# A two-layer cross-attention and feed-forward kernel: its first stage in another order, and GpSimd's first query splits moved

## The chip, the cores and the metric

The kernel runs on one core of one Trainium2 chip. The metric is the device time of one execution in microseconds (us); lower is better. The core has TensorE (PE; its weight loads are shown apart as PEld), VectorE (DVE), ScalarE (ACT), GpSimd (POOL) and SyncE (SP, which here only issues DMAs). Each takes its own instructions in the order in which they are written and waits on semaphores that the program names.

## The reference, cut to what matters

```python
x = x + fake_quant(layernorm(x)) @ fake_quant(ctx)                      # first attention, 0..255 levels
x = x + mx_linear(silu(mx_linear(ln(x), w_gate)) * mx_linear(ln(x), w_up), w_down)   # fp6 rows, fp4 weights, blocks of 32
x = x + attention(ln(x) @ wq, rope(ctx @ wk), ctx @ wv, mask) @ wo       # 32 query heads, 8 key heads of 128
x = x + (silu(ln(x) @ gate * s) * (ln(x) @ up * s)) @ down * s
```

x is 2 x 256 x 512, ctx is 2 x 512 x 512, the inner width of both feed-forward layers is 1376 (padded to 1408), everything float32.

## The kernel before, in words

The keys and values of the second attention depend on ctx alone, so they fill TensorE in the first stage, while the other engines quantise.

**Stage one** (to about 130 us). TensorE computes 27 units of keys and values: `("k", i, b)` is key head i for batch b, `("v", i, h)` is 128 context rows i by 512 columns h; a unit is four float32 matmuls of 128x512. The table STEPS (L39) names them in order, as a first and a second part of each of 8 steps. Their results go round three PSUM banks (5, 6, 7; `rotation`, `take`, L269 and L462): a unit can begin when the unit three places before it has been copied out by ScalarE (`copy_keys`, `copy_values`) and from there SP stores it to DRAM. Beside that the 33 weight tiles of the first feed-forward layer (gate, up, down) are quantised to fp4 in 9 chunks, 8 of four tiles and a last one of one tile. For chunk i: SP `mx_load(i)`; DVE `mx_peaks`, `mx_exponents`; POOL `scale_in(i)`; ACT `mx_lift(i, 0)` and `(i, 1)`; DVE `mx_round(i, 0)`, `(i, 1)`, `mx_clip(i)`; POOL `scale_out(i)`, which lets TensorE transpose the chunk in two halves (`mx_turn(i, 0)`, `(i, 1)`, L491) that ACT keeps in WT (`mx_keep`). The rows of x go through `quantise_rows` (a layernorm on DVE), `rows_scale`, `clip_rows`, `rows_keep`; the context through `context_scale`, `clip_context`, `context_keep`; `attention0(b)` is the first attention for batch b. Then DVE normalises the result (`layernorm`), `fp6` quantises it, POOL's `fp6_out` writes it, TensorE turns it (`turn_quantised(1)`) and ACT keeps it. The key head 0 needs its rotary embedding at once: ACT copies the swapped halves out (`swap`), DVE multiplies by the cosine in PSUM (`key_cosine`), POOL by the sine (`key_sine`), DVE adds (`key_rotate`). The other heads are rotated later.

**Stage two** (about 132 to 184 us) is the first feed-forward layer for four row tiles t: TensorE `gate_up(t)` in three slices c (PSUM banks 4 to 7 in pairs, so that slice n waits until DVE has read slice n-2), ACT `silu(t)`, DVE `inter_products(t)` and `inter_quantise(t)` (fp6 again), POOL `fp6_out`, TensorE `turn_inter(t)`, ACT `keep_inter(t)`, TensorE `down(t)`, DVE `add_down(t)`. Five key units that stage one has no room for (LATE_KEYS) are put in its gaps as `late_keys(n, parts)`; late_keys(3) computes head 7, batch 0, and stands between the transposes of row tiles 2 and 3 (`turn_rows`, L622). It waits for `wk_in`, the load of that head's weights, `k_load(7)` (L421). DVE's last layernorm normalises tiles 0 to 2 and then tile 3.

**Stage three** (from 185 us) is the second attention, one software pipeline over units U; POOL splits each query weight in a high and a low part (`split`, L1070; `wqh_ready`, `wq_split`), and SP loads head h of wq only after `wq_split` has reached h-1 (two raw buffers). SP's queue at the end of stage two reads, in this order:

```python
            wq_load(2, 0)
            wq_load(3, 1)
            k_load(7)
            for i, b in LATE_KEYS[:4]:
                key_store(i, b)
            sp.wait_ge(ffn0_done, NT)
```

with `after(sp, wq_split, h - 1)` inside wq_load. The fourth layer (660 us on) is the last feed-forward.

## Time and profile before

| | us |
|---|---|
| median of 3 runs | 709.29 (708.45 to 712.96) |
| the profiled execution, its own time | 712.11 |
| its span from the first to the last recorded instruction | 710.0 |
| busy in the span: PE, DVE, POOL, ACT | 672.4, 525.8, 457.6, 362.8 |

2.1 us of the execution's own time lie around the span. Row times below are in us from the span's start, the duration follows the start, and brackets at a row's end give the idle time before it and what ended it. A group "x8" is several instructions of one kind in a row.

### The profile page before, as it was taken

What the parts mean: (1) busy time and instruction counts of PE and PEld (TensorE: products, weight loads), DVE (VectorE), ACT (ScalarE), POOL (GpSimd) and SP (SyncE); (2) the same over time, 40 slices, a digit from 0 to 9 for tenths busy, and PEclk for the clock granted to TensorE, in tenths of its full rate; (3) what the DMA queues carried; (4) which work ended last, traced back from release to release, by engine and by line L of the source; (5) the groups of instructions that cost most, each with busy time, mean ns of one, the idle gap of its engine ahead of it and who ended that gap; (6) DMA issues with size and microseconds to landing.
All of it is one profiled execution on the core that took longest, in us unless ns stands there. A gap on an engine that the chain in (4) does not pass through costs nothing.

```text
span 710.0 us, 10983 instructions
## 1 busy us (share of the span) xinstructions
PE 672.4 (95%) x3099; PEld 494.8 (70%) x3104; DVE 525.8 (74%) x1039; ACT 362.8 (51%) x684; POOL 457.6 (64%) x401
## 2 busy tenths in 40 slices
PE   4989899899989999999999999999999999699998
PEld 2434344444566788888888888888888887588886
DVE  4977799778678888888889888888888885631113
ACT  2659444542466666665665665565665663211111
POOL 2365716424269879778878779689688554556661
PEclk9989999999999999999999999999999999999999
DMA  9885322140232113023132141221221021122221
GB/s 338 274 309 184 127 90 75 45 163 18 98 109 80 68 61 118 31 66 112 30 101 77 37 126 44 83 80 44 88 74 40 21 65 55 54 81 89 89 89 60
DMA packets 39402, 67.25 MB, mean 95 GB/s; under 512 B 3664, under 2 KB 11984, under 8 KB 38352
## 3 DMA queue, kind: packets, MB, share of 16 engines
q1 hardware_dynamic: 39376, 66.93, 28.8%
q8 instruction: 13, 0.21, 0.1%
q14 instruction: 13, 0.11, 0.0%
HBM read 57.48 MB, written 9.44 MB: 94 GB/s over the span
## 4 chain that ended last, share of the span: by engine, by line
PE 77%; DVE 10%; issue 4%; POOL 4%; ACT 3%; DMA 1%; SPq 0%; POOLq 0%; ACTq 0%; DVEq 0%
PE ps L635 16%; PE ps L637 16%; PE ps L636 16%; PE ps L703 11%; PE ps L668 7%; PE ps L503 4%; PE ps L519 4%; PE ps L566 2%; DMA X<-in_x 1%; DVE mx_amax L1244 1%; DVE mx_raw L1262 1%; DVE f L1292 1%; DVE f_amax L1287 1%; POOL wq_sb L1074 1%; PE ps L497 1%
## 5 line engine op out<-in xcount | busy, mean ns | idle before, releaser
L1083 POOL TENSOR_SCALAR prob<-prob,rinv 128x512 f32<-128x512 f32 x128 | 89.4, 699 | 79.3 <-DVE rinv L1420 79.3
L944 ACT ACTIVATE prob<-ps,nmax 128x512 f32<-128x512 f32 x128 | 88.3, 690 | 97.4 <-DVE nmax L1413 94.9
L703 PE MATMUL ps<-xt,wq_sb 128*128 128x512 f32 x384 | 103.2, 393 | 3.8 <-DVE q_cos L1428 2.1
L955 ACT CAST pT<-ps 128x512 fp32r<-128x512 f32 x128 | 75.1, 587 | 52.0 <-PE ps L668 51.0
L1413 DVE CUSTOM_DVE_ANT_0 ps<-ps,mask_sb 128x512 f32<-128x512 f32 x128 | 87.9, 686 | 6.7 <-PE ps L637 6.3
L1434 DVE TENSOR_TENSOR pT<-ps,pT 128x512 fp32r<-128x512 f32 x128 | 86.3, 674 | 2.6 <-ACT pT L955 1.7
L703 PEld LDWEIGHTS ps<-xt,wq_sb 128*128 128x128 f32 x384 | 71.6, 188 | 21.9 <-issue 4.6
L668 PE MATMUL ps<-idf,prob 128*128 128x128 f32 x512 | 76.7, 272 | 0.3 <-POOL prob L1083 0.3
L668 PEld LDWEIGHTS ps<-idf,prob 128*128 128x128 f32 x512 | 63.8, 141 | 17.0 <-POOL prob L1083 1.0
L503 PE MATMUL ps<-ctxT,wk_sb 128*128 128x512 f32 x128 | 63.4, 636 | 7.7 <-DMA ctxT<-in_ctx_cols 6.7
L1035 POOL TENSOR_TENSOR mx_raw<-mx_raw,mx_r 128x2048 f32<-128x2048 f32 (+1 forms) x9 | 30.2, 3354 | 61.4 <-DVE mx_r L1252 61.4
L519 PE MATMUL ps<-wv_sb,ctxT 128*128 128x512 f32 x128 | 58.8, 610 | 5.3 <-DVE col L1228 2.8
L635 PE MATMUL ps<-pT,vt 128*128 128x512 f32 x128 | 61.1, 477 | 0.5 <-DVE pT L1434 0.5
L1086 POOL TENSOR_TENSOR q_swp<-q_swp,ropeQ 128x512 f32<-128x512 f32 x32 | 47.1, 1472 | 17.6 <-ACT q_swp L965 17.6
L1470 DVE SCALAR_TENSOR_TENSOR int<-ps,sc,silu 128x512 f32<-128x512 f32 x11 | 8.2, 750 | 59.6 <-PE ps L637 59.6
L635 PE MATMUL ps<-wo_sb,oT 128*128 128x512 f32 x128 | 50.2, 393 | 1.7 <-DVE oT L1401 1.4
L635 PE MATMUL ps<-kt,qt 128*128 128x512 f32 x128 | 50.6, 395 | 0.9 <-DVE kt L1447 0.5
L637 PE MATMUL ps<-pT,vt 128*128 128x512 f32 x128 | 50.8, 397 | 0.0
L636 PE MATMUL ps<-pT,vt 128*128 128x512 f32 x128 | 50.3, 393 | 0.0
L637 PE MATMUL ps<-kt,qt 128*128 128x512 f32 x128 | 50.2, 392 | 0.0
L1074 POOL TENSOR_TENSOR wo_sb<-wo_raw,wo_sb 128x512 fp32r<-128x512 f32 x32 | 48.4, 1511 | 2.7
L636 PE MATMUL ps<-wo_sb,oT 128*128 128x512 f32 x128 | 50.0, 391 | 0.0
(152 smaller groups left out, 1572.2 us busy)
## 6 DMA issues: line engine op xcount, KB each, us to landing
mx_raw<-in_mxw SPq DMA_DIRECT2D x8, 1024.0 KB, 6.7
wq_raw<-in_wq SPq DMA_DIRECT2D x32, 256.0 KB, 3.1
wo_raw<-in_wo SPq DMA_DIRECT2D x32, 256.0 KB, 2.7
k_scr<-k_st SPq DMA_DIRECT2D x16, 256.0 KB, 2.0
v_scr<-v_st SPq DMA_DIRECT2D x16, 256.0 KB, 2.3
kr<-k_scr SPq DMA_DIRECT2D x16, 256.0 KB, 2.9
vr<-v_scr SPq DMA_DIRECT2D x16, 256.0 KB, 3.7
kr_swp<-k_scr SPq DMA_DIRECT2D x28, 128.0 KB, 3.3
```

The source lines that it names most:

```text
L503: last = mm(bank(n), wk_sb[:, i % 2, k], ctxT[:, k, b * CTX:(b + 1) * CTX], start=(k == 0), stop=(k == KD - 1))
L519: last = mm(bank(n), ctxT[:, k, i * P:(i + 1) * P], wv_sb[:, k, h * 512:(h + 1) * 512], start=(k == 0), stop=(k == KD - 1))
L635: mm(out_ap, left[0], right[0], start=first, stop=False)
L636: mm(out_ap, left[0], right[1], start=False, stop=False)
L637: return mm(out_ap, left[1], right[0], start=False, stop=final)
L668: last = nc.tensor.transpose(bank(2 + i % 2)[:, k * P:(k + 1) * P], prob[:, i, k * P:(k + 1) * P], idf[:])
L703: last = mm(query_bank(H), wq_sb[:, par, l, k], xt[:, r, k], start=(n == 0), stop=(n == 11))
L944: nc.scalar.activation(prob[:, j], bank(j % 2), ACT.Exp, bias=nmax[:, j:j + 1], scale=-1.0, accum_out=rsum[:, j:j + 1]).then_inc(exps, 1)
L955: copy(pT[:, v % 2, 0, :, i * P:(i + 1) * P], bank(2 + i % 2).rearrange("p (k c) -> p k c", k=4)).then_inc(ph_ready, 1)
L1083: nc.gpsimd.tensor_scalar(prob[:, i], prob[:, i], rinv[:, i:i + 1], 1.0, ALU.mult, ALU.mult).then_inc(probs, 1)
L1413: nc.vector.tensor_tensor_reduce(out=bank(j % 2), in0=bank(j % 2), in1=mask_sb[:, 2 * (u % 2) + j % 2], scale=-1.0, scalar=BIG, op0=ALU.ad ...
L1434: tt(pT[:, v % 2, 1, :, i * P:(i + 1) * P], bank(2 + i % 2).rearrange("p (k c) -> p k c", k=4), pT[:, v % 2, 0, :, i * P:(i + 1) * P].bitc ...
```

## The change

It has four parts.

1. **Loads.** SP issues x and the first half of wv ahead of the first weight chunk, then chunks 0 and 1, and the context rows as two loads of 1 MB (`ctx_load`) in place of one of 2 MB. DVE does quantise_rows before mx_peaks(0).
2. **Banks, units and the first key head.** STEPS is written anew: step 1 has four units, the last step has two, and its second part is empty. The rotation of key head 0 goes from DVE and PSUM to POOL and SBUF: ACT makes one more copy (`k_own`), which frees the PSUM bank, and POOL does all three operations (`key_rotate`, one for each batch); the result has its own buffer and its own store.
3. **Gate and up ahead of chunk 6.** In step 7 no chunk is transposed; mx_turn(6, 0), (6, 1) come behind gate_up(0), and mx_turn(7, 0), (7, 1), (8, 0) behind gate_up(1). POOL does the fp6_out of the rows before scale_out(6), DVE does mx_round(8, 0) before mx_clip(7), and attention0 before the peaks of a chunk.
4. **GpSimd's query splits.** The split of query head 0 goes ahead of the last fp6_out of stage two. Behind it POOL waits for `ln_ready` 12, which is the last row tile's normalisation, before it splits head 1. late_keys(2) gives one of its four parts to the place ahead of down(3), and three behind it, where it was two and two.

```diff
-    ([("v", 0, 1), ("v", 1, 1)], [("k", 1, 0)]),
-    ([("k", 1, 1), ("v", 2, 1)], [("k", 2, 0)]),
...
-    ([("v", 7, 0), ("v", 7, 1)], [("k", 5, 0)]),
+    ([("v", 0, 1), ("v", 1, 1), ("k", 1, 0)], [("k", 1, 1)]),
+    ([("v", 2, 1), ("k", 2, 0)], [("v", 3, 1)]),
...
+    ([("v", 7, 1), ("k", 5, 0)], []),
...
             k_load(0)
             ctxT_load(0)
-            mx_load(0)
             sp.dma_start(X[:], x.rearrange("(t p) d -> p t d", p=P)).then_inc(x_in, 16)
             sp.dma_start(sc[:], scalars).then_inc(sc_in, 16)
             wv_load(0)
+            mx_load(0)
+            mx_load(1)
             sp.dma_start(idf[:], ident).then_inc(id_in, 16)
-            mx_load(1)
+            ctxT_load(1)
             sp.dma_start(ropeK[:], rope_k).then_inc(rk_in, 16)
-            ctxT_load(1)
+            wv_load(1)
             mx_load(2)
-            wv_load(1)
             k_load(1)
-            key_store(0, 0)
+            ctx_load(0)
...
-                if i > 0:
+                if 0 < i < NFULL - 1:
                     mx_turn(i - 1, 0)
...
             gate_up(0)
+            mx_turn(NFULL - 2, 0)
+            mx_turn(NFULL - 2, 1)
+            gate_up(1)
+            mx_turn(NFULL - 1, 0)
             late_keys(0, range(0, 2))
-            mx_turn(NFULL - 1, 0)
             mx_turn(NFULL - 1, 1)
-            gate_up(1)
             mx_turn(NFULL, 0)
             late_keys(0, range(2, 4))
...
             turn_inter(NT - 1)
-            late_keys(2, range(0, 2))
+            late_keys(2, range(0, 1))
             down(NT - 1)
-            late_keys(2, range(2, 4))
+            late_keys(2, range(1, 4))
...
             swap(0)
+            copy_values(0, 0)
+            copy_values(1, 0)
             mx_lift(0, 0)
             mx_lift(0, 1)
+            rows_scale()
+            copy_values(2, 0)
...
             mx_lift(1, 1)
+            swap(1)
             rows_keep()
-            swap(1)
...
+            def key_rotate(b):
+                if b == 0:
+                    pool.wait_ge(rk_in, 16)
                 pool.wait_ge(k_swapped, b + 1)
+                pool.wait_ge(*keys_out(0, b))
                 tt(k_swp[:, b], k_swp[:, b], ropeK[:, 1], ALU.mult).then_inc(k_sined, 1)
+                tt(k_own[:, b], k_own[:, b], ropeK[:, 0], ALU.mult).then_inc(k_cosed, 1)
+                pool.wait_ge(k_sined, b + 1)
+                pool.wait_ge(k_cosed, b + 1)
+                tt(k_own[:, b], k_own[:, b], k_swp[:, b], ALU.add).then_inc(k_roped, 1)
...
-                scale_out(i)
                 if i == L0_AT + 2:
                     fp6_out(q1[:].rearrange("p t d -> p (t d)"), NT * D, 0, q1_ready)
+                scale_out(i)
+                if i == 0:
+                    key_rotate(1)
             scale_out(NFULL)
...
+            for t in range(NT):
+                if t == NT - 1:
+                    pool.wait_ge(wq_in[0], 16)
+                    split(wq_sb[:, 0, 0], wq_sb[:, 0, 1], wq_raw[:, 0], wqh_ready, wq_split, 1)
+                after(pool, intq_turned, t - 1)
+                fp6_out(int_q[:, t % 2], IPAD, t + 1, intq_ready)
...
-            pool.wait_ge(wq_in[0], 16)
-            split(wq_sb[:, 0, 0], wq_sb[:, 0, 1], wq_raw[:, 0], wqh_ready, wq_split, 1)
+            pool.wait_ge(ln_ready, 3 * NT)
             pool.wait_ge(rq_in, 16)
```

POOL at the end of stage two, before (int_q is written by fp6_out, wq_sb by a split):

```order
L1046 TENSOR_TENSOR int_q<-f6c,f_e 128x1408 [waits f6_clipped,intq_turned] x2
L1072 TENSOR_SCALAR wq_sb<-wq_raw 128x512 [waits wq_in0]
L1074 TENSOR_TENSOR wq_sb<-wq_raw,wq_sb 128x512 [waits wqh_ready]
L1072 TENSOR_SCALAR wq_sb<-wq_raw 128x512 [waits rq_in,wq_in1]
L1074 TENSOR_TENSOR wq_sb<-wq_raw,wq_sb 128x512 [waits wqh_ready]
```

and now:

```order
L1069 TENSOR_TENSOR int_q<-f6c,f_e 128x1408 [waits f6_clipped,intq_turned]
L1097 TENSOR_SCALAR wq_sb<-wq_raw 128x512 [waits wq_in0]
L1099 TENSOR_TENSOR wq_sb<-wq_raw,wq_sb 128x512 [waits wqh_ready]
L1069 TENSOR_TENSOR int_q<-f6c,f_e 128x1408 [waits f6_clipped,intq_turned]
L1097 TENSOR_SCALAR wq_sb<-wq_raw 128x512 [waits wq_in1,ln_ready,rq_in]
L1099 TENSOR_TENSOR wq_sb<-wq_raw,wq_sb 128x512 [waits wqh_ready]
```

The first split has moved ahead of the last int_q, and the second now waits for ln_ready as well. SP at the same place stands as it did (this is the new kernel; wk_sb is k_load(7), the two wq_raw are heads 2 and 3):

```order
L389 DMA wq_raw<-in_wq 128x512 [waits wq_split] x2
L319 DMA wk_sb<-in_wk 128x512 [waits k_sums]
L324 DMA k_scr<-k_st 128x512 [waits k_copied] x4
L389 DMA wq_raw<-in_wq 128x512 [waits wq_split,ffn0_done]
L394 DMA wo_raw<-in_wo 128x512
```

Nothing moved on it. TensorE from the first gate_up on, before (L566 is gate_up, L503 a key part, L497 mx_turn):

```order
L566 MATMUL ps<-WT,q1T 128x384 [waits inter_ready]
L566 MATMUL ps<-WT,q1T 128x384 x7
L503 MATMUL ps<-ctxT,wk_sb 128x512 [waits wk_in1]
L503 MATMUL ps<-ctxT,wk_sb 128x512
L497 MATMUL ps<-idb,mx_w 128x128 [waits mx_kept,mx_ready]
L497 MATMUL ps<-idb,mx_w 128x128 x7
L497 MATMUL ps<-idb,mx_w 128x128 [waits mx_kept,mx_ready]
L497 MATMUL ps<-idb,mx_w 128x128 x7
L566 MATMUL ps<-WT,q1T 128x512 [waits inter_ready]
```

and now, from the last slice of gate_up(1) (L577 is gate_up, L513 a key part, L507 mx_turn, L585 turn_inter):

```order
L577 MATMUL ps<-WT,q1T 128x384 [waits inter_ready]
L577 MATMUL ps<-WT,q1T 128x384 x7
L507 MATMUL ps<-idb,mx_w 128x128 [waits mx_kept,mx_ready]
L507 MATMUL ps<-idb,mx_w 128x128 x7
L513 MATMUL ps<-ctxT,wk_sb 128x512 [waits wk_in1]
L513 MATMUL ps<-ctxT,wk_sb 128x512
L507 MATMUL ps<-idb,mx_w 128x128 [waits mx_kept,mx_ready]
L507 MATMUL ps<-idb,mx_w 128x128 x7
L507 MATMUL ps<-idb,mx_w 128x128 [waits mx_kept,mx_ready]
L507 MATMUL ps<-idb,mx_w 128x128 x3
L513 MATMUL ps<-ctxT,wk_sb 128x512 x2
L585 MATMUL ps<-idb,int_q 128x128 [waits intq_ready,mx_kept]
```

What stood between gate_up(0) and gate_up(1), a half of late_keys(0) and chunk 7, now stands between gate_up(1) and turn_inter(0).

## Rows read from the trace of the kernel before

**Rows 1.** Stretches: length, busy of PE, PEld, DVE, ACT, POOL, PEclk, DMA, GB/s.

```profile
0.00:130.00 130.00, 114.54 (x382) 53.25 (x384) 104.81 (x150) 67.24 (x80) 64.09 (x25) 0.96 0.56 193
...
44.00:46.00 2.00, 2.00 (x3) 0.67 (x2) 1.19 (x1) 0.00 (x0) 0.00 (x0) 0.50 0.86 246
```

**Rows 2.** TensorE's timeline in stage one, each row behind a wait; the last is gate_up(0).

```profile
6.65 5.75 PE L503 MATMUL ps<-ctxT,wk_sb 128*128 128x512 f32 x8 [6.65 <-DMA ctxT<-in_ctx_cols]
14.84 14.00 PE L519 MATMUL ps<-wv_sb,ctxT 128*128 128x512 f32 x32 [2.44 <-DMA wv_sb<-in_wv]
...
41.42 0.91 PE L497 MATMUL ps<-idb,mx_w 128*128 128x128 bf16 x8 [2.29 <-POOL mx_w L1041]
43.34 6.19 PE L503 MATMUL ps<-ctxT,wk_sb 128*128 128x512 f32 x8 [1.01 <-DVE k_st L1282]
...
79.12 5.37 PE L519 MATMUL ps<-wv_sb,ctxT 128*128 128x512 f32 x8 [2.81 <-DVE col L1228]
...
132.07 4.93 PE L566 MATMUL ps<-WT,q1T 128*128 128x512 bf16 x24 [2.09 <-ACT q1T L790]
```

**Rows 3.** GpSimd's timeline: scale_in(2), scale_out(0); scale_out(6), the rows' fp6_out.

```profile
34.03 3.64 POOL L1035 TENSOR_TENSOR mx_raw<-mx_raw,mx_r 128x2048 f32<-128x2048 f32 x1 [6.59 <-DVE mx_r L1252]
37.64 3.64 POOL L1041 TENSOR_TENSOR mx_w<-mx_q,mx_e 128x2048 bf16<-128x2048 bf16 x1
...
119.92 3.64 POOL L1041 TENSOR_TENSOR mx_w<-mx_q,mx_e 128x2048 bf16<-128x2048 bf16 x1
123.52 3.64 POOL L1046 TENSOR_TENSOR q<-f6c,f_e 128x2048 bf16<-128x2048 bf16 x1
```

**Rows 4.** VectorE in stage two: the first products of row tiles 1 and 2.

```profile
143.35 0.69 DVE L1345 TENSOR_TENSOR int<-silu,ps 128x512 f32<-128x512 f32 x1
...
151.96 1.27 DVE L1345 TENSOR_TENSOR int<-silu,ps 128x512 f32<-128x512 f32 x2
```

**Rows 5.** VectorE's last layernorm: a step beside a split; tile 3, first and last.

```profile
175.02 1.12 DVE L1184 TENSOR_TENSOR newton<-newton,var_eps 128x3 f32<-128x3 f32 x1
...
178.92 0.68 DVE L1354 TENSOR_TENSOR X<-ps,X 128x512 f32<-128x512 f32 x1
...
182.70 0.55 DVE L1187 TENSOR_SCALAR xhat<-X,meanvar,rstd 128x512 f32<-128x512 f32 x1
```

**Rows 6.** TensorE's timeline: late_keys(3), then the transposes of tile 3.

```profile
180.11 3.60 PE L503 MATMUL ps<-ctxT,wk_sb 128*128 128x512 f32 x8
183.54 0.60 PE L629 MATMUL ps<-idf,xhat 128*128 128x128 f32 x4
```

**Rows 7.** VectorE's timeline: the starts of two layernorms, then mx_clip(7) and mx_clip(8).

```profile
11.99 2.47 DVE L1165 BATCH_NORM_STATS2 stats<-X 128x6 f32<-128x512 f32 x4 [0.21 <-DMA X<-in_x]
...
97.83 2.47 DVE L1165 BATCH_NORM_STATS2 stats<-X 128x6 f32<-128x512 f32 x4
...
123.65 4.06 DVE L1270 TENSOR_SCALAR mx_q<-mx_q 128x2048 bf16<-128x2048 bf16 x1
...
129.07 2.51 DVE L1270 TENSOR_SCALAR mx_q<-mx_q 128x512 bf16<-128x512 bf16 x1
```

**Rows 8.** Timelines in stage two: mx_turn(7, 1), its copy on ScalarE, turn_inter(0).

```profile
140.35 0.61 PE L497 MATMUL ps<-idb,mx_w 128*128 128x128 bf16 x8 [1.19 <-ACT WT L820]
...
140.99 1.01 ACT L820 COPY WT<-ps 128x1024 bf16<-128x1024 bf16 x1 [0.79 <-PE ps L497]
...
147.54 0.78 PE L574 MATMUL ps<-idb,int_q 128*128 128x128 bf16 x11
```

**Rows 9.** Timelines of GpSimd's second split and of SP; DMAs from 176.4 us: KB, us to landing.

```profile
174.16 0.62 POOL L1072 TENSOR_SCALAR wq_sb<-wq_raw 128x512 fp32r<-128x512 f32 x1
174.85 1.27 POOL L1074 TENSOR_TENSOR wq_sb<-wq_raw,wq_sb 128x512 fp32r<-128x512 f32 x1
...
176.52 0.43 SPq L317 DMA_DIRECT2D wk_sb<-in_wk  x1
...
wk_sb<-in_wk SPq DMA_DIRECT2D x1, 256.0 KB, 3.1
```

More of the change, by code:

```diff
@@ L208, in build @@
             res = sb("res", [P, NT, D], F32, a)
-        x_in, id_in, sc_in, ctx_in = sem("x_in"), sem("id_in"), sem("sc_in"), sem("ctx_in")
+        x_in, id_in, sc_in = sem("x_in"), sem("id_in"), sem("sc_in")
+        ctx_in = [sem(f"ctx_in{i}") for i in range(2)]
         ctxT_in = [sem(f"ctxT_in{i}") for i in range(2)]
@@ L285, in keys_out @@
         def keys_out(i, b):
-            n = 2 * i + b
-            return (k_roped, n + 1) if i == 0 else (k_copied, n - 1)
+            return k_copied, 2 * i + b + 1
         def drained(unit):
@@ L342, in wv_load, with ctx_load @@
                              wv[:, n * 512:(n + 1) * 512].rearrange("(k p) c -> p k c", p=P)).then_inc(wv_in[n], 16)
+            def ctx_load(b):
+                rows = slice(b * CTX, (b + 1) * CTX)
+                sp.dma_start(ctx_f[:, 4 * b:4 * b + 4], ctx_rows[rows, :].rearrange("(t p) d -> p t d", p=P)).then_inc(ctx_in[b], 16)
             k_load(0)
             ctxT_load(0)
-            mx_load(0)
             sp.dma_start(X[:], x.rearrange("(t p) d -> p t d", p=P)).then_inc(x_in, 16)
@@ L366, in _ @@
                     mx_load(i + NRAW)
+                if i == 1:
+                    for b in range(2):
+                        sp.wait_ge(k_roped, b + 1)
+                        sp.dma_start(k_scr[0, b], k_own[:, b]).then_inc(k0_stored, 16)
                 stores(STEPS[i][0] + STEPS[i][1])
@@ L805, in swap @@
                 act.wait_ge(k_sums, b + 1)
-                n = 0 if b == 0 else rotating(("k", 0, b))
+                n = key_bank(0, b)
                 copy(k_swp[0:64, b], ps[64:128, n * 512:(n + 1) * 512])
                 copy(k_swp[64:128, b], ps[0:64, n * 512:(n + 1) * 512]).then_inc(k_swapped, 1)
+                copy(k_own[:, b], bank(n)).then_inc(k_copied, 1)
             def copy_values(i, h):
@@ L879, in _ @@
                 mx_lift(i + 1, 0)
-                copy_unit(STEPS[i][0][1])
-                if i + 1 < NFULL:
-                    mx_lift(i + 1, 1)
+                if i == 1:
+                    copy_unit(STEPS[i][0][1])
+                    context_scale(0)
+                for unit in STEPS[i][0][2 if i == 1 else 1:]:
+                    copy_unit(unit)
+                if i == NFULL - 1:
+                    break
+                mx_lift(i + 1, 1)
+                if i in (2, 3):
+                    context_keep(i - 2)
                 mx_keep(i - 1, 0)
@@ L909, in _ @@
             silu(0)
+            mx_keep(NFULL - 2, 0)
+            mx_keep(NFULL - 2, 1)
+            silu(1)
             mx_keep(NFULL - 1, 0)
             mx_keep(NFULL - 1, 1)
-            silu(1)
             mx_keep(NFULL, 0)
@@ L1270, in mx_clip @@
                 ts(mx_q[:, p, 0:n], mx_q[:, p, 0:n], 1.5, -1.5, ALU.min, ALU.max).then_inc(mx_rounded, 1)
-            def key_cosine(b):
-                n = 0 if b == 0 else rotating(("k", 0, b))
-                dve.wait_ge(rk_in, 16)
-                dve.wait_ge(k_swapped, b + 1)
-                tt(bank(n), bank(n), ropeK[:, 0], ALU.mult).then_inc(k_cosed, 1)
-            def key_rotate(b):
-                n = 0 if b == 0 else rotating(("k", 0, b))
-                dve.wait_ge(k_cosed, b + 1)
-                dve.wait_ge(k_sined, b + 1)
-                tt(k_st[:, b], bank(n), k_swp[:, b], ALU.add).then_inc(k_roped, 1)
             def fp6(src, n):
@@ L1299, in fp6_clip @@
                 ts(f6c[:, 0:n], f6[:, 0:n], 7.5 / 64, -7.5 / 64, ALU.min, ALU.max).then_inc(f6_clipped, 1)
+            quantise_rows()
             mx_peaks(0)
             mx_exponents(0)
-            quantise_rows()
             mx_peaks(1)
@@ L1307, in _ @@
                 mx_round(i, 0)
-                if i < 2:
-                    key_cosine(i)
                 mx_round(i, 1)
-                if i < 2:
-                    key_rotate(i)
+                if i in (L0_AT, L0_AT + 1):
+                    attention0(i - L0_AT)
                 if i + 2 <= NFULL:
@@ L1321, in _ @@
                     clip_context(1)
-                if i == L0_AT:
-                    attention0(0)
                 if i == L0_AT + 1:
-                    attention0(1)
                     dve.wait_ge(l0_done, NT)
@@ L1334, in _ @@
                     mx_exponents(i + 2)
-            mx_round(NFULL, 0)
             mx_clip(NFULL)
```

51 lines of the change are left out of this document (22 added, 29 removed), and 8 rows, old and new, of the table STEPS.

## The prediction

> **What bounds the kernel now.** Read first the stretches. Up to 130 us TensorE is busy for 114.5 us [rows 1], so it was kept waiting for 15.5. Read then, on its timeline, what ended each wait [rows 2]. Beside the first load (6.7 us, which stays) it is 2.4 for wv, 2.3 for the first chunk's weights (POOL), 1.0 for the rotated key of batch 1 (DVE) and 2.8 for VectorE to read the first attention's sums. Two of these stops cost more than themselves. Behind the one at 41 us the granted clock is 0.50, which is 1.2 of 2.4 GHz [rows 1], and one unit takes 6.19 us, where four units took 14.0, 3.5 each [rows 2]: 2.7 lost. Behind the one of 2.81 us a unit takes 5.37: 1.9 lost. TensorE is what a microsecond of stage one is paid in. It is not alone: gate_up(0) at 132.07 waits for ScalarE's copy of the turned rows, and these for POOL's fp6_out, which ended at 127.2 [rows 2, 3].
>
> In stage two VectorE is the bound. It goes product, fp6, product, fp6: tile 1 began 11.3 us and tile 2 19.9 us behind gate_up(0)'s start [rows 4]. At the stage's end two chains meet: VectorE's last normalised tile is there at 183.25 [rows 5], and late_keys(3) on TensorE ends at 183.54 [rows 6]. From 185 us on TensorE paces itself and nothing in the change touches that stretch, so the shift that stands at 185 us stands at the end.
>
> **The first loads.** Ahead of wv stands one megabyte less; it comes in the place of x, which landed at 12.0 [rows 7]. The first key unit ends at 12.4 (14.84 less 2.44), so the wait of 2.4 goes.
>
> **Chunk 0 and the first key head.** TensorE now does one unit more before mx_turn(0, 0). It was free for it at 39.1 (41.4 less 2.3); less 2.4, plus 3.5, it is 40.1. What is late next? quantise_rows starts some 3 us earlier, as x is in where chunk 0 was, but chunk 0's exponents now come behind it. That costs chunk 0 about as much as VectorE saves by that start and by giving its multiplications and additions of the key away. Following both, scale_out(0), which ended at 41.3 [rows 3], ends at 40.9. So the stop is 0.8, and the 1.0 for the key and the slow clock's 2.7 go. GpSimd gets six operations for the key, of the length of the second half of a split (1.3 us), where it had two; they stand in stretches where it waited for VectorE, 6.6 us ahead of scale_in(2) alone [rows 3]. I take them as hidden; the first rival is what happens if they are not.
>
> **ScalarE** now has the context's scaling ahead of a chunk's copies. I count short stops at mx_turn(0, 1), 1.5, (1, 1), 1.6, (2, 1), 0.8, and 1.0 for chunk 5's weights. They are estimates from following ScalarE's list by its copies of 0.6 and 1.0 us, and each may be 0 to 2. The stop of 2.09 at 130 us did not slow what came behind it (24 matmuls in 4.93 us, 0.2 each) [rows 2], so I put no clock on these.
>
> **attention0.** Behind it TensorE waited 2.8 until VectorE, busy with a chunk's peaks, read the bank, and lost 1.9 by the clock. VectorE now reads first: 4.7 gone.
>
> **Chunk 6 put off.** Its two halves leave TensorE's path here: 0.9 us, as a half is recorded with 0.61 and the next work begins 0.45 behind its start [rows 8].
>
> The sum for TensorE: turn_quantised(1) ended at 130.0 (132.07 less 2.09). Less 2.4, 3.3, 2.7, 4.7 and 0.9 (14.0), plus the stops that I expect (0.8, 1.5, 1.6, 0.8, 1.0: 5.7), it is 121.7. The other path: fp6_out ends 3.6 earlier, since scale_out(6) now comes behind it [rows 3], and about 2.9 more, since the second layernorm, at 97.8 before [rows 7], starts at about 94.9: 127.2 becomes 120.7, when TensorE begins these transposes. Both agree. gate_up(0) waited 2.1 for ScalarE; 0.9 of that was chunk 6's copy, and a key's copy of 0.5 comes in: 1.7. So 121.7 + 1.7 = 123.4, **8.7 us earlier** (bounds: 10, if most short stops are not there, and 4, if the clock falls once more and a stop doubles).
>
> **Stage two.** What stood between gate_up(0) and (1) now stands behind gate_up(1), whose last slice must wait for VectorE's first product of tile 1. That stays 11.3 behind gate_up(0) and lasts to 12.0. Counting on: the slice, 1.5, to 13.5; mx_turn(7, 0) 13.9; half a key, 1.7, 15.6; mx_turn(7, 1) 16.1; ScalarE's copy of it, 1.0 [rows 8], 17.3; mx_turn(8, 0) 17.5; the other half key 19.3; turn_inter(0), 0.6, 19.9; first slice of gate_up(2) 21.7; silu 22.3. VectorE is free at 19.9 and began tile 2 there [rows 4]; now it begins at 22.4. The next slices come close behind, and the tile's last product ends 2.7 late. Later tiles find TensorE ahead again. **2.7 us given back** (between 1 and 3.5). The shift is then -6.0.
>
> VectorE's mx_clip(8) may be held up. mx_clip(7) took 4.06 us beside fp6_out, and mx_clip(8), of a quarter of its size, 2.51 [rows 7]; each ended when GpSimd's operation beside it did. I take nothing here, since mx_clip(8) now follows directly on mx_clip(7), for which scale_out(7) waits: VectorE should be first. The Trainium skill has a rule for it (SBUF — State Buffer, "SBUF: two separate sides"): VectorE in a 2-port mode and GpSimd take one port pair under an exclusive lock, and whichever starts first keeps it for its whole instruction. These rows agree. By that rule all hangs on who is first, and if it is GpSimd the sum is that of the second rival.
>
> **The splits.** The first, ahead of the last fp6_out, fits in GpSimd's wait for VectorE. The second no longer lies beside the layernorm of tiles 0 to 2, where a step took 1.12 [rows 5] that takes 0.16 by itself; with that and two smaller ones some 1.9 us go, and down(3) is done in time, as one of late_keys(2)'s parts has left the place ahead of it. In before's time the last tile is normalised at 181.3, not 183.25.
>
> But three queues hang on the second split. POOL begins it only when `ln_ready` is 12, behind that last tile. SP's wq_load(3, 1) waits for its result, and k_load(7) stands behind it in SP's queue. late_keys(3) on TensorE waits for that load, and behind it stand tile 3's transposes and all queries. Before, the split ended at 176.1, k_load(7) was issued at 176.52 and landed 3.1 later [rows 9], at 179.6, half a microsecond ahead of late_keys(3) at 180.11 [rows 6]. Now, in before's time: 181.3; the split 2.0 (174.16 to 176.12); SP 0.4; landing 3.1: 186.8. TensorE comes there at about 180.7 and stands still for 6.1 us, with nothing else that it may do. Then late_keys(3), 3.4 at the full clock. The stops of 2.3 and 2.8 us in stage one were followed by half the clock; this one is longer, so I add 2.4, between their 1.9 and 2.7. That is 192.6; the transposes, 0.6, end at 193.2, where they ended at 184.1. **9.1 us lost** (6.7 if the clock stays up; 10.8 if all of it runs at half).
>
> **The sum.** -8.7 + 2.7 + 9.1 = +3.1 us. On the profiled execution's own 712.1 that is 715.2. This execution lies 2.8 above the median of the runs, 709.3, so I predict **712.4**. A measurement tells a change of 1%, about 7.1 us, from none.
>
> **The rivals.**
> *GpSimd is late with chunk 0 (slower).* The key's rotation for batch 0 stands ahead of scale_in(2), that for batch 1 ahead of scale_in(3), and VectorE's clips can wait beside them as mx_clip(7) did. If scale_out(0) ends 2.3 us or more behind TensorE, at 42.4 or later, the stop is what it was, and with it the clock's 2.7; the stop itself gives back 1.5, and mx_clip(1), held beside the batch 1 rotation, 1.2. Of 8.7 stay 3.3, and the sum is +8.5: 717.8. Against it: GpSimd is busy for 64 of 130 us [rows 1]. 0.15.
> *mx_clip(8) is locked out.* The first product of stage two then waits until scale_out(7) has ended, up to 2.7: 715.1. For it: two clips of that kind waited before. 0.17.
> *The load is no bound.* k_load(7) comes in time, or the stretch ahead of 185 us has slack that I don't see. Then -8.7 + 2.7 = -6.0, plus 0.6 for late_keys(2)'s part that now stands behind down(3): 703.9. Against it: SP's queue, and that VectorE and TensorE end within 0.3 us of each other before. 0.08, of which 0.04 below 702.2 with all stops of stage one gone.
> *The forecast:* 0.60, by itself 708.5 to 716.
>
> The range is 706.0 to 717.5: below it lies most of the third rival, above it half of the first. Faster by over 1% (under 702.2) 0.04; slower by over 1% (over 716.4) 0.17, the first rival and a little of the second; within 1% 0.79.
>
> **What would show it.** TensorE waits some 6 us for the DMA of wk_sb ahead of late_keys(3), near 175 us in the new kernel's own time, with PEclk at 0.5 behind it, and GpSimd's second split stands behind VectorE's last xhat. gate_up(0) comes at about 123.4, with no wait for wv, at most 1 us for the first chunk and none for col. VectorE is idle for 2.5 us ahead of tile 2's products. It would be wrong if that wait is under 3 us, if gate_up(0) is later than 128, or if stage three differs by itself.

## The result, and the profile after

The changed kernel takes **714.67 us** (median of 15 runs, 714.17 to 715.71). The kernel before took 712.15 beside it (15 runs, 708.18 to 713.57): ratio 1.0052, 95% interval 1.0039 to 1.0065. That is slower by half a per cent, inside the 1% that the forecast called no change. 712.4 was forecast, with 706.0 to 717.5 as its range.

The profiled execution took 715.59; its span is 713.0, against 710.0 before. The stretches, with the columns of [rows 1]:

```profile
0.00:130.00 130.00, 115.94 (x413) 54.36 (x416) 106.25 (x151) 72.92 (x88) 71.91 (x30) 1.00 0.57 197
40.00:46.00 6.00, 5.10 (x25) 2.26 (x24) 5.93 (x6) 5.94 (x6) 5.86 (x5) 1.00 0.64 246
178.00:186.00 8.00, 5.78 (x8) 2.52 (x9) 0.00 (x0) 0.00 (x0) 0.00 (x0) 0.57 0.41 156
```

The clock fell behind two stops of stage one before and behind none now; it is low at 178 to 186 instead, where VectorE, ScalarE and GpSimd do nothing at all. TensorE's timeline, which answers to [rows 2] and [rows 6] ("..." stands for rows left out):

```profile
12.34 13.90 PE L529 MATMUL ps<-wv_sb,ctxT 128*128 128x512 f32 x32
...
30.07 7.13 PE L529 MATMUL ps<-wv_sb,ctxT 128*128 128x512 f32 x16 [0.39 <-ACT v_st L833]
...
41.17 0.61 PE L507 MATMUL ps<-idb,mx_w 128*128 128x128 bf16 x8 [0.54 <-POOL mx_w L1064]
...
45.63 0.61 PE L507 MATMUL ps<-idb,mx_w 128*128 128x128 bf16 x8 [0.36 <-ACT WT L838]
...
58.95 0.61 PE L507 MATMUL ps<-idb,mx_w 128*128 128x128 bf16 x8 [0.96 <-ACT WT L838]
...
71.00 0.61 PE L507 MATMUL ps<-idb,mx_w 128*128 128x128 bf16 x8 [0.58 <-ACT WT L838]
...
107.70 0.62 PE L507 MATMUL ps<-idb,mx_w 128*128 128x128 bf16 x8 [1.50 <-POOL mx_w L1064]
...
121.69 4.93 PE L577 MATMUL ps<-WT,q1T 128*128 128x512 bf16 x24 [1.61 <-ACT q1T L803]
...
128.25 0.61 PE L507 MATMUL ps<-idb,mx_w 128*128 128x128 bf16 x8 [1.19 <-ACT WT L838]
...
134.09 1.47 PE L577 MATMUL ps<-WT,q1T 128*128 128x384 bf16 x8 [1.77 <-DVE int L1360]
...
139.42 0.38 PE L507 MATMUL ps<-idb,mx_w 128*128 128x128 bf16 x4 [1.19 <-ACT WT L838]
...
172.26 1.47 PE L642 MATMUL ps<-idf,xhat 128*128 128x128 f32 x12
180.22 6.04 PE L513 MATMUL ps<-ctxT,wk_sb 128*128 128x512 f32 x8 [6.49 <-DMA wk_sb<-in_wk]
186.10 0.60 PE L642 MATMUL ps<-idf,xhat 128*128 128x128 f32 x4
```

The waits for wv (2.44) and for col (2.81) are gone, that for chunk 0's weights is 0.54 instead of 2.29, and gate_up(0) starts at 121.69 instead of 132.07. Then the new wait: 6.49 us for the load of wk_sb, and late_keys(3) takes 6.04 where it took 3.60. VectorE ahead of tile 2's products [rows 4], its last normalised tile [rows 5], GpSimd's second split and SP's two loads behind it [rows 9]:

```profile
144.59 0.69 DVE L1360 TENSOR_TENSOR int<-silu,ps 128x512 f32<-128x512 f32 x1 [2.69 <-ACT silu L923]
...
173.68 0.55 DVE L1218 TENSOR_SCALAR xhat<-X,meanvar,rstd 128x512 f32<-128x512 f32 x1
```
```profile
174.44 0.62 POOL L1097 TENSOR_SCALAR wq_sb<-wq_raw 128x512 fp32r<-128x512 f32 x1 [9.41 <-DVE xhat L1218]
175.15 1.26 POOL L1099 TENSOR_TENSOR wq_sb<-wq_raw,wq_sb 128x512 fp32r<-128x512 f32 x1
...
157.95 18.82 SPq L389 DMA_DIRECT2D wq_raw<-in_wq  x2
176.81 0.43 SPq L319 DMA_DIRECT2D wk_sb<-in_wk  x1
```

Read the last four rows as one chain: xhat done at 174.23, the split to 176.41, SP stands in its queue for 18.8 us until then, k_load(7) is issued at 176.81 and TensorE can use it at 180.22. The turn of row tile 3 ends at 186.70, where it ended at 184.14.

### The profile page after: what moved, and what is told of

Its sections match the earlier page's. It is cut to its first block, busy times and chain, and to the rows that moved or that the text cites. A ratio compares the mean times of both kernels' runs of the same rounds, so it can differ in the third digit from the quotient of the medians.

```text
span 713.0 us, 10987 instructions
## 1 busy us (share of the span) xinstructions
PE 671.0 (94%) x3099; PEld 494.0 (69%) x3104; DVE 520.4 (73%) x1035; ACT 363.9 (51%) x686; POOL 463.8 (65%) x405
## 4 chain that ended last, share of the span: by engine, by line
PE 71%; POOL 9%; DVE 9%; issue 8%; ACT 2%; DMA 1%; SPq 0%; POOLq 0%; ACTq 0%; DVEq 0%
PE ps L648 16%; PE ps L650 16%; PE ps L649 16%; PE ps L716 11%; PE ps L681 7%; POOL mx_raw L1058 3%; POOL mx_w L1064 3%; PE ps L577 2%; PE ps L513 1%; DMA X<-in_x 1%; PE ps L529 1%; DVE f L1311 1%; DVE f_amax L1306 1%; DVE stats L1196 1%; DVE mx_amax L1275 1%
## 5 line engine op out<-in xcount | busy, mean ns | idle before, releaser
L513 PE MATMUL ps<-ctxT,wk_sb 128*128 128x512 f32 x128 | 63.0, 634 | 13.3 <-DMA ctxT<-in_ctx_cols 6.8
L529 PE MATMUL ps<-wv_sb,ctxT 128*128 128x512 f32 x128 | 57.2, 596 | 0.4 <-ACT v_st L833 0.4
L513 PEld LDWEIGHTS ps<-ctxT,wk_sb 128*128 128x128 f32 x128 | 25.3, 204 | 40.7 <-issue 33.3
L648 PE MATMUL ps<-wo_sb,oT 128*128 128x512 f32 x128 | 50.3, 393 | 1.7 <-DVE oT L1416 1.4
```

What stands on the lines that cost most here:

```text
L513: last = mm(bank(n), wk_sb[:, i % 2, k], ctxT[:, k, b * CTX:(b + 1) * CTX], start=(k == 0), stop=(k == KD - 1))
L529: last = mm(bank(n), ctxT[:, k, i * P:(i + 1) * P], wv_sb[:, k, h * 512:(h + 1) * 512], start=(k == 0), stop=(k == KD - 1))
L648: mm(out_ap, left[0], right[0], start=first, stop=False)
```

## The experiments

Ten kernels and the changed one once more, measured in three groups on three chips. The kernel before was run beside each group and had medians of 710.06, 711.91 and 712.23 us. So a ratio is a kernel's time over that of the kernel before in the same group, and what an edit does is read from positions in the traces. "The turn's end" below is the end of tile 3's transposes, behind which no edit reaches.

### Is it the queue behind the second split?

**The load put first**: SP issues k_load(7) ahead of the loads that wait for the split.

```diff
+            k_load(7)
             wq_load(2, 0)
             wq_load(3, 1)
-            k_load(7)
```

> The changed kernel, with one line moved: SP issues the load of key head 7's weights ahead of the loads of query heads 2 and 3 instead of behind them. Theory A (the second split holds SP's queue, and through it this load and TensorE): the wait of 6.5 us for wk_sb and the slow clock's 2.4 behind it go; late_keys(3) begins near 173.6, at once and at the full clock, the turn of row tile 3 ends near 177.7 instead of 186.7, and the time is 9.0 lower than the changed kernel's 714.67: about 705.6, 6.5 under the kernel before. Rival B (the wait on TensorE is only a cover: another thing, such as the last layernorm or the late first query split, ends the stage nearly as late, or the clock falls all the same): the turn ends no earlier than 180 and the time is 708 or more. Rival C (the load is slow by itself, for instance beside the stores): the wait for wk_sb stays, moved or shortened by under 3 us, and the time is over 711.

Measured 708.12 us, ratio 0.996 (0.9938 to 0.9982). TensorE at the place in question:

```profile
172.20 1.47 PE L642 MATMUL ps<-idf,xhat 128*128 128x128 f32 x12
173.51 3.60 PE L513 MATMUL ps<-ctxT,wk_sb 128*128 128x512 f32 x8
176.95 0.60 PE L642 MATMUL ps<-idf,xhat 128*128 128x128 f32 x4
```

No wait stands in front of late_keys(3), it takes 3.60 again, and the turn's end is 177.55: 9.15 us earlier, with 9.0 expected. GpSimd's wait and split are where they were (174.40), so the wait itself holds nobody but SP. The stage does what theory A says; the whole time moved by less than 9, which a later section takes up.

**The wait alone**, in the kernel before:

```diff
             pool.wait_ge(wq_in[0], 16)
             split(wq_sb[:, 0, 0], wq_sb[:, 0, 1], wq_raw[:, 0], wqh_ready, wq_split, 1)
+            pool.wait_ge(ln_ready, 3 * NT)
```

> The kernel before, with one line added: GpSimd waits for the last row tile's normalisation ahead of the second query split (part 4's wait alone; nothing else of the change). Theory A: the split moves from 174.2 to behind 181.3 to 183.3, SP's load of key head 7's weights behind it, TensorE waits some 6 to 7 us for wk_sb and has the lower clock behind it; the turn of row tile 3 ends near 192 to 194 instead of 184.1 and the time is 8 to 10 above the kernel before's 712.15: 720 to 722. It would be about 1.8 less than that if VectorE, freed of the split beside it, ends its layernorm earlier. Rival B (the wait costs nothing by itself; the loss in the changed kernel comes from its other parts): the same as before within 2 us.

Measured 721.48 us, ratio 1.015 (1.0121 to 1.018): 10.7 us by the ratio. GpSimd and SP, then TensorE:

```profile
178.11 0.62 POOL L1072 TENSOR_SCALAR wq_sb<-wq_raw 128x512 fp32r<-128x512 f32 x1 [7.95 <-DVE xhat L1188]
...
170.19 10.24 SPq L379 DMA_DIRECT2D wq_raw<-in_wq  x2
180.47 0.43 SPq L317 DMA_DIRECT2D wk_sb<-in_wk  x1
```
```profile
76.77 3.70 PE L519 MATMUL ps<-wv_sb,ctxT 128*128 128x512 f32 x8 [2.82 <-DVE col L1229]
...
128.05 4.93 PE L566 MATMUL ps<-WT,q1T 128*128 128x512 bf16 x24 [2.09 <-ACT q1T L790]
...
183.96 5.64 PE L503 MATMUL ps<-ctxT,wk_sb 128*128 128x512 f32 x8 [7.72 <-DMA wk_sb<-in_wk]
189.44 0.60 PE L629 MATMUL ps<-idf,xhat 128*128 128x128 f32 x4
```

The same chain, with nothing else of the change: rival B is out. The trace shows a second thing. Stage one is the kernel before's, the stop of 2.82 us for col stands in it, yet the unit behind it takes 3.70 and not 5.37, and gate_up(0) starts at 128.05 and not at 132.07. **The slow clock behind the two stops of stage one was a matter of the execution, not of the kernel.** (The stop at 41 us is 1.81 here and was 2.29; the one for col is the same to 0.01.) Counted from an execution without it, the turn's end moves from 184.14 less 4.02, 180.1, to 190.04: 9.9 us.

**The wait away**, and **all of part 4 undone**:

```diff
-            pool.wait_ge(ln_ready, 3 * NT)
```

> The changed kernel without GpSimd's wait for the last normalisation ahead of the second split; the first split stays ahead of the last fp6_out. Theory A: the split runs near 163 to 168, as soon as fp6_out(3) is done and the load is in, the load of wk_sb is in time, and all of the stall and the slow clock goes: about 705.6, equal to the kernel with the load put first within 1 us. The split may lie beside VectorE's layernorm of tiles 0 to 2 and delay it by 1 to 2, but late_keys(3) on TensorE ends at about 177 anyway, which hides it. Rival D (the layernorm is the chain that matters, which is what the wait was for): 1 to 2 us slower than the kernel with the load put first.

> The changed kernel with all of part 4 undone: both splits behind the last fp6_out, no wait for the last normalisation, late_keys(2) two parts ahead of down(3) and two behind. Theory A, in which parts 1 to 3 are worth 10 us less 3 in stage two: about 705, 9 to 10 lower than the changed kernel and within 1 us of the kernel with the load put first. So part 4 as a whole brings nothing even where its harm is taken away, if A is right; a rival E (moving the first split and the part of late_keys(2) is a gain of about 2, by the 1.8 that VectorE no longer loses beside a split) has it 1 to 2 us slower than the kernel with the load put first.

Measured 707.25 us, 0.9949 (0.9924 to 0.9974), and 706.48 us, 0.9929 (0.9902 to 0.9956). The turn ends at 177.67 and 177.64, as with the load put first (177.55). Rivals D and E are out. With all of part 4 undone, both splits lie beside VectorE's layernorm: its var_eps takes 0.83 and a Newton step 1.12, where alone they take 0.17 and 0.16, and its last tile is done at 176.75 instead of 174.18 (0.8 of it is that VectorE comes to this layernorm later). But late_keys(3) on TensorE holds the transposes of that tile until 177.04 in that kernel and hides all of it. The 1.8 us that part 4 saves VectorE are worth nothing here.

### How much of the 9 us reaches the whole time?

The changed kernel itself, once more, beside the next three:

> The changed kernel itself, unchanged, beside the others of this call on one chip. With the load of wk_sb put first, the turn of row tile 3 ended 9.15 us earlier in the profile, but its runs' median, beside another chip's runs of the kernel before, was only 6.6 lower than the changed kernel's. Theory: the step is 9 in the stage and the rest is a slow stretch of the granted clock behind the last layernorm (608 us on), whose length differs from execution to execution; then the medians of this kernel and of the next one differ by 9 less 0 to 2.5, and the positions at 187 us by 9 exactly. Rival: the load put first costs something in the stretch between 185 and 600 us; then positions there drift apart again.

Measured 714.83 us (713.78 to 716.62), ratio 1.0058 (1.0036 to 1.008), as in the first measurement. Its stall is 6.54 and its turn's end 187.03, 9.5 behind the kernel with the load first. The medians are 6.7 apart, and the ratios (1.0058 and 0.996, from two groups) 0.0098, which is 7.0 us. The stretch behind the last layernorm tells where the rest is. TensorE in the profile of the changed kernel, and then in that of the kernel with the load first:

```profile
615.16 3.54 PE L642 MATMUL ps<-idf,xhat 128*128 128x128 f32 x16 [4.74 <-DVE xhat L1218]
```
```profile
606.04 3.35 PE L642 MATMUL ps<-idf,xhat 128*128 128x128 f32 x16 [4.74 <-DVE xhat L1218]
```

The two are still 9.12 us apart here, as they were 9.15 apart at the turn's end, so nothing between 187 and 606 us gives the gain back, and the rival is out. In every profile TensorE waits 4.74 or 4.75 us at this place and its clock is low behind that, but not for equally long. The kernel with the load first, 600 to 612 us, and below it the kernel with both gains (the last experiment), each in its one profiled execution:

```profile
600.00:612.00 12.00, 6.40 (x30) 5.21 (x29) 9.20 (x25) 3.20 (x5) 5.66 (x7) 0.86 0.20 66
```
```profile
600.00:612.00 12.00, 9.26 (x32) 7.74 (x33) 5.37 (x14) 3.89 (x6) 5.42 (x5) 0.57 0.23 74
```

A mean of 0.86 over 12 us is 3.4 us at 0.50, one of 0.57 is 10.3. The kernel with the load first shows both: three of its twelve runs have a mean granted clock of 0.998 and take 705.9 to 706.2 us, the other nine have 0.993 and take 708 to 709.7. The changed kernel spends about 7 us at half clock beside its stall and, by its mean clocks, mostly the short stretch at the end. So some 2 of the 9 us are lost again behind 606 us, in the runs with the long stretch. What decides between the short and the long one is not settled by any run here.

### Where do the 3 us of stage two go?

**Another order on TensorE**, on top of the load put first. ScalarE's copy of chunk 7's first half goes ahead of silu(1) with it.

```diff
             mx_turn(NFULL - 2, 0)
+            late_keys(0, range(0, 1))
             mx_turn(NFULL - 2, 1)
-            gate_up(1)
+            late_keys(0, range(1, 2))
             mx_turn(NFULL - 1, 0)
-            late_keys(0, range(0, 2))
+            gate_up(1)
             mx_turn(NFULL - 1, 1)
+            late_keys(0, range(2, 3))
             mx_turn(NFULL, 0)
-            late_keys(0, range(2, 4))
+            late_keys(0, range(3, 4))
```

> The kernel with the load put first (708.12 us; its profile had gate_up(0) at 121.62 and tile 2's first product at 144.53), and in stage two another order on TensorE: the four parts of late_keys(0) one by one between the transposes of the chunks, and the first half of chunk 7 ahead of gate_up(1), so that they fill the stops of 1.2 and 1.8 us that TensorE had there; ScalarE's copy of that half goes ahead of silu(1). Theory A (the 2.7 to 3.2 given back in stage two are TensorE's own order): turn_inter(0) at 138.3 instead of 141.36, tile 2's first product at 141.9 instead of 144.53, when VectorE is free; the end of tile 3's turn at 174.8 to 175.0 instead of 177.55, and the time 2.6 lower: about 705.5. Rival B (TensorE catches up by itself, and the bound is elsewhere, such as the last key units on TensorE): tile 2 starts earlier, but the turn of tile 3 ends less than 1 us earlier. Rival C (ScalarE's copy ahead of silu(1) delays the products of tile 1): no gain, or up to 1 slower.

Measured 705.70 us, ratio 0.9929 (0.9904 to 0.9954). TensorE, and VectorE at tile 2's first product:

```profile
128.32 0.61 PE L507 MATMUL ps<-idb,mx_w 128*128 128x128 bf16 x8 [0.28 <-ACT WT L840]
...
130.12 0.61 PE L507 MATMUL ps<-idb,mx_w 128*128 128x128 bf16 x8 [0.28 <-POOL mx_w L1066]
130.56 5.06 PE L577 MATMUL ps<-WT,q1T 128*128 128x512 bf16 x24
...
137.26 0.38 PE L507 MATMUL ps<-idb,mx_w 128*128 128x128 bf16 x4 [0.28 <-ACT WT L840]
...
138.40 0.78 PE L585 MATMUL ps<-idb,int_q 128*128 128x128 bf16 x11
```
```profile
141.87 0.68 DVE L1362 TENSOR_TENSOR int<-silu,ps 128x512 f32<-128x512 f32 x1
```

The stops of 1.19, 1.77 and 1.19 have become three of 0.28 (the last slice of gate_up(1) is now part of the x24), VectorE has no idle time left ahead of tile 2, and the turn's end is 174.74 against 177.55. All three positions of theory A came within 0.1. What the change put behind gate_up(1) had cost 2.7 to 2.8 us, as TensorE's own order and not for want of data.

### Which edits of stage one are worth something?

**The sums read behind the peaks again**, on top of the load put first:

```diff
-                if i in (L0_AT, L0_AT + 1):
-                    attention0(i - L0_AT)
                 if i + 2 <= NFULL:
                     mx_peaks(i + 2)
+                if i in (L0_AT, L0_AT + 1):
+                    attention0(i - L0_AT)
```

> The kernel with the load put first (gate_up(0) at 121.62), with one thing of part 3 undone: VectorE reads the first attention's sums behind the peaks of the next chunk again, not ahead of them. Theory A (this is what took away TensorE's stop of 2.8 us, and a microsecond of TensorE is one of stage one): a stop of 2 to 2.8 us comes back on TensorE near 73 us, gate_up(0) comes 2 to 2.8 later, or up to 4.7 if the clock falls behind the stop; time 2 to 3 higher, about 710.5. Rival B (VectorE, which now waits 1.96 and 1.22 us for these sums with the peaks behind it, is as much the bound as TensorE): VectorE gains up to 3.2, gate_up(0) moves by under 1 us either way, and the time is the same.

Measured 705.20 us, ratio 0.992 (0.9895 to 0.9946). Theory A is wrong: of the stop that the order was to take away nothing comes back. Rival B named the right wait, but put its worth at nothing. The order was a loss: VectorE had waited for the sums, and with the peaks behind it lost that time. VectorE with the load first, and then here:

```profile
72.44 0.81 DVE L1259 TENSOR_SCALAR col<-ps,sx 128x512 f32<-128x512 f32 x1 [1.96 <-PE ps L493]
...
86.28 0.81 DVE L1259 TENSOR_SCALAR col<-ps,sx 128x512 f32<-128x512 f32 x1 [1.22 <-PE ps L493]
```
```profile
73.07 0.80 DVE L1259 TENSOR_SCALAR col<-ps,sx 128x512 f32<-128x512 f32 x1
...
87.65 0.80 DVE L1259 TENSOR_SCALAR col<-ps,sx 128x512 f32<-128x512 f32 x1
```

TensorE's stop for chunk 5's weights, 1.50 at 107.70 in the changed kernel, is gone, and gate_up(0) starts at 120.76, 0.86 earlier, though the first load landed 0.3 later: 1.2 us gained by undoing an edit. The median fell by more, 2.9 us. All six runs have a mean clock of 0.995 or 0.998, so by their clocks none has the longest slow stretch at the end, which nine of the twelve runs with the load first have; the rest of the 2.9 lies there.

**The same order in the kernel before**, where VectorE reads the sums ahead of the peaks:

> The kernel before, with one thing of part 3: VectorE reads the first attention's sums ahead of the next chunk's peaks. The question is what took away TensorE's stop of 2.8 us at 77 to 79, since undoing this order in the new kernel did not bring the stop back. Theory A (in the kernel before VectorE is later against TensorE, so there the order counts): the sums are read some 2.2 earlier, the stop shrinks from 2.8 to under 0.8, gate_up(0) comes about 2 earlier, up to 3.9 where the stop's slow clock goes with it. Rival B (VectorE is the bound there as well and only gives back the peaks' time later): gate_up(0) moves by under 0.7, and the time is the same.

Measured 710.57 us, ratio 0.9982 (0.9957 to 1.0007).

```profile
43.39 5.24 PE L503 MATMUL ps<-ctxT,wk_sb 128*128 128x512 f32 x8 [1.32 <-DVE k_st L1282]
...
76.03 3.70 PE L519 MATMUL ps<-wv_sb,ctxT 128*128 128x512 f32 x8 [0.62 <-DVE col L1228]
...
109.81 0.62 PE L497 MATMUL ps<-idb,mx_w 128*128 128x128 bf16 x8 [1.50 <-POOL mx_w L1041]
```

The stop shrinks from 2.82 to 0.62, so the order counts there; and a stop of 1.50 for chunk 5's weights appears, which the kernel before has not. gate_up(0) starts at 128.65; without the 1.54 that the unit at 43 us lost by the clock it is 127.1, against 128.05. So 0.9 remains of 2.2, which the ratio can't tell from nothing.

What took the stop away in the new kernel is seen where both kernels have the old order. In the trace with the wait alone, whose stage one is the kernel before's, TensorE's sums are done at 72.23 and VectorE reads them 3.7 us behind:

```profile
75.92 0.80 DVE L1229 TENSOR_SCALAR col<-ps,sx 128x512 f32<-128x512 f32 x1
```

In the new kernel with the old order they are done at 72.88, and VectorE reads them at 73.07 (above), 0.2 behind. So VectorE is 2.8 us earlier through the other edits, and that is enough for the stop to stay away; which of them made it earlier was not taken apart further.

**The loads alone**: part 1's first loads and quantise_rows first, in the kernel before.

> The kernel before, with the order of the first loads of part 1 (x and the first half of wv ahead of the weight chunks) and quantise_rows ahead of the first peaks; units, banks and the key's rotation as before. Theory A (TensorE's 2.4 us of waiting for wv go, but without a unit more in step 1 they only turn into waiting for chunk 0's weights): TensorE starts the v units at 12.4, and its stop at mx_turn(0, 0) grows from 1.8 to 2.3 to about 5; gate_up(0) within 0.7 of the kernel before, time the same, or up to 2.7 different by the clock behind that stop. Rival B (the earlier loads carry through): gate_up(0) 2.4 earlier and the time 2.4 lower.

Measured 711.12 us, ratio 1.0008 (0.9983 to 1.0033).

```profile
12.70 10.46 PE L519 MATMUL ps<-wv_sb,ctxT 128*128 128x512 f32 x24
26.68 6.49 PE L519 MATMUL ps<-wv_sb,ctxT 128*128 128x512 f32 x8 [3.52 <-ACT v_st L815]
...
43.31 0.61 PE L497 MATMUL ps<-idb,mx_w 128*128 128x128 bf16 x8
```
```profile
23.85 1.97 ACT L828 ACTIVATE ps<-mx_raw 128x1024 f32<-128x1024 f32 x2 [9.78 <-POOL mx_raw L1035]
25.85 0.30 ACT L867 CAST idb<-idf 128x128 bf16<-128x128 f32 x1
26.05 0.58 ACT L815 COPY v_st<-ps 128x512 f32<-128x512 f32 x1
```

The wait for wv goes and brings nothing, as theory A has it, but the new stop comes at another place. The fourth v unit waits 3.52 us for its bank, because ScalarE's copy of the first one stands in its list behind mx_lift(0), which waits 9.78 for GpSimd. Behind the stop the clock is low, and the unit takes 6.49 instead of 3.5. So TensorE comes to mx_turn(0, 0) at 43.31 and waits for nothing there, as scale_out(0) has ended at 42.65. Without the stop for the bank it would have waited at chunk 0: it was free for it at 39.1 in the kernel before, 2.1 less is 37.0, and 5.7 us are missing to 42.65. This is an estimate from these rows, and it is what theory A expected, about 5.

The change has two more edits for these two places: two copies ahead of mx_lift(0), and a unit more ahead of mx_turn(0, 0). In its trace the stop for the bank is 0.39 and that for chunk 0 is 0.54. By the estimate the copies alone would only move the wait to chunk 0. Neither was run by itself with the loads.

**scale_out(6) first on GpSimd**, on top of the load put first:

```diff
-                if i == L0_AT + 2:
-                    fp6_out(q1[:].rearrange("p t d -> p (t d)"), NT * D, 0, q1_ready)
                 scale_out(i)
+                if i == L0_AT + 2:
+                    fp6_out(q1[:].rearrange("p t d -> p (t d)"), NT * D, 0, q1_ready)
```

> The kernel with the load put first, with one thing of part 3 undone: GpSimd does scale_out(6) ahead of the fp6_out of the rows again. Theory A (the rows' fp6_out ended 0.96 us ahead of TensorE's turn, which is what this order is worth): fp6_out ends at 121.7 instead of 118.06, TensorE's turn at 121.75 instead of 118.95, gate_up(0) at about 124.4, and the time is 2.7 higher, about 710.8; VectorE's wait of 3.06 us ahead of chunk 8's second multiplication goes, and buys nothing. Rival B (that wait of VectorE delays the first products of stage two, so its end makes good for half or more): gate_up(0) is later, but tile 0's products are under 1.4 later, and the time is under 1.4 higher.

Measured 712.46 us, ratio 1.0003 (0.9982 to 1.0025), 4.3 above the kernel with the load first.

```profile
121.63 1.89 PE L484 MATMUL ps<-idb,q 128*128 128x128 bf16 x16 [2.58 <-POOL q L1069]
124.68 6.68 PE L577 MATMUL ps<-WT,q1T 128*128 128x512 bf16 x24 [1.17 <-ACT q1T L803]
```

TensorE's turn waits 2.58 us and gate_up(0) starts at 124.68, as theory A has it with 121.75 and 124.4. Behind that stop the clock is low in this execution (these transposes take 1.89 instead of 1.06, gate_up(0) 6.68 instead of 4.93), and the turn's end is 182.35: 4.8 later, where theory A named 2.7. 3.1 of it is there when gate_up(0) starts, and the rest is mostly the slow clock in it. Of the single edits tried in stage one this order is the one worth most.

### Both gains together

> The kernel with the load of wk_sb put first, with the other order in stage two (that alone: 705.70 us, the turn of tile 3 ends at about 174.8 against 177.55) and with the sums read behind the peaks again (that alone: 705.20 us; gate_up(0) 14.28 us behind the start of key unit (1, 1)'s... in plain words 0.86 earlier, and 1.4 earlier counted from TensorE's first matmul). Theory A (both are on the path and add): gate_up(0) at 120.2 to 120.8, the turn of tile 3 ends at 173.4 to 174.0, time 1.4 under the kernel with the other order alone and 3 under the one with the sums alone: about 703.5. Rival B (only one of the two counts, because the stage is then bound by what both have in front of them): the better of the two, 705.2.

Measured **704.07 us** (702.13 to 704.34), ratio 0.9901 (0.9868 to 0.9935). gate_up(0) starts at 120.44 and the turn's end is 173.46, 4.1 ahead of the kernel with only the load first; the two add. Against the changed kernel's 186.70 it is 13.2 earlier. Of its six runs four have the mean clock 0.993, and the profiled one of them has the long slow stretch at 600 us (above); the run with 0.998 took 702.13. So the time is less than 13.2 lower. It beats the kernel before by 1% and the changed one by some 1.5%.

## Why the prediction was right, and where its steps were not

The measured column is read from the profiles of the two kernels. From gate_up(0)'s start to the turn's end it is 52.07 us before and 65.01 now, 12.94 more. The last product of tile 2 starts 22.66 behind gate_up(0) before and 25.81 now, which is the 3.2 of the second line; the third line is the rest of the 12.94.

| step | predicted | measured |
|---|---|---|
| gate_up(0), against 132.07 | -8.7 | -10.4 |
| given back in stage two | +2.7 | +3.2 |
| the stall, less VectorE's earlier end, and the clock | +9.1 | +9.8 |
| the shift at the turn's end | +3.1 | +2.6 |

**The queue of the second split** was right in its mechanism, its place and its size: a stall of 6.1 and 2.4 by the clock were forecast, 6.49 and 2.44 came. Five kernels bear it out: the changed kernel has the stall, taking away either the wait or the place in the queue takes it away (three kernels), and the wait alone makes it.

**The first loads.** "So the wait of 2.4 goes" is true, and the step rightly went on to ask who is late next at chunk 0. But it looked only at GpSimd's and VectorE's side, and left out who frees TensorE's banks. With the loads alone the fourth v unit waits 3.52 us for ScalarE's copy; the change also puts two copies ahead of mx_lift(0), which the step did not name, and the wait is 0.39.

**Chunk 0** was right: a stop of 0.54 for 0.8, and GpSimd's six operations are hidden. So the first rival did not come, though scale_in(3) begins the moment the second rotation ends and VectorE's three operations beside that rotation take 0.98 to 1.26 us.

**ScalarE's stops** were forecast as 1.5, 1.6, 0.8 and for chunk 5 1.0; they are 0.36, 0.96, 0.58 and 1.50, with 0.39 for v_st. Together with chunk 0's stop these are 4.3 us for the 5.7 that were added, which is most of the 1.7 that gate_up(0) came earlier than forecast. The one that is larger, chunk 5's, is made by the next step.

**attention0** is the step that failed: "VectorE now reads first: 4.7 gone". The stop of 2.8 went, but not by this: undone in the new kernel, it stays away, and the edit costs 1.2. The step took the cause from the edit that names it, and did not follow VectorE against TensorE up to that point. Measured, VectorE reads 3.7 us behind the sums in the kernel before, and 0.2 behind in the new kernel with the old order; and the second layernorm's start, 94.9 by the forecast, came at 92.38, so VectorE had gained more than the step counted.

**The slow clock of stage one** was put down in full as a gain, 1.9 behind this stop and 2.7 behind chunk 0's. It was no property of the kernel: in an execution of the same stage without it, gate_up(0) starts at 128.05. At equal clock the change gains 6.4 us in stage one, not 8.7 or 10.4, and at the turn's end it loses 6.6 (186.70 against 180.1), not 3.1 or 2.6. That the sum and the measured shift agree is in part luck: the sum was made on an execution with 4.0 us of this slow clock, and the kernel before's runs have it often enough that their median lies as high. Beside the experiments its times go from 707.2 us, at a mean clock of 0.998, to 715.1, at 0.986; the changed kernel was never under 713.8.

**Stage two** was right in cause, and the experiment recovered it to a tenth. The 12.0 us to the last slice of gate_up(1) were 12.4 (134.09 less 121.69), and the first product of tile 2 came 22.9 behind gate_up(0) for 22.4. Of the two stops of 1.19 between transposes the second was counted, as ScalarE's copy; the first costs nothing there, since TensorE waits 1.77 for VectorE behind it.

**mx_clip(8)** was not locked out; the second rival did not come. mx_clip(7) and (8) take 0.89 for the two, and begin at 122.42, ahead of scale_out(7) at 123.18. (The reading that each clip before ended when GpSimd's operation did is a little off: they ended 0.55 and 0.15 behind it.) What stands there is a wait that no step named: VectorE stood still for 3.06 us, until 121.81, because mx_round(8, 0) writes the buffer that scale_out(6) still reads. It cost nothing, since VectorE was free again 1.0 us ahead of the first product.

**The splits' gain for VectorE** (1.9) came, and is worth nothing with or without the stall.

**The last step, from the profiled execution to the median**, is what made the number 2.3 too low. The sum on the profiled execution was 715.2, and the changed kernel's profiled execution took 715.59. Then 2.8 were taken off, because that execution lay above the median of three runs, 709.3. But three runs are few for a kernel whose runs differ by 5 us: with 15 its median is 712.15, and the profiled execution, 712.11, lies on it. And the changed kernel has no slow clock in stage one that could be missing in other runs; its 15 runs lie within 1.5 us of one another. There was nothing to take off.

## What to carry to other kernels

Ahead of a new wait, list what is queued behind it on its engine, and then who waits on those: here the load that mattered was two queues away, and moving one line gave back 9 us of the stage. A stop that goes away in a change with many edits is not yet explained by the edit that names it; follow both engines to that point, or undo the edit alone: here the first loads brought nothing by themselves, and the order of the sums cost 1.2 us. And where a profiled execution holds slow clock behind a stop, ask whether other executions of the same kernel have it too, and whether the stop is there in the new kernel, before counting the slow clock as a gain or carrying that execution's distance from the median over.
